# Slot attention's scan: the normalisation of a slot's probabilities moves behind score 2 of the next slot in VectorE's order

## The reference

```python
def step(carry, xs):                       # over 512 tokens, 16 heads, 2 sequences
    Sk, Sv = carry
    q_t, k_t, v_t, w_t, g_t, b_t = xs
    gt = jnp.exp(g_t)
    bw = b_t[:, :, None] * w_t
    Sk = Sk * gt[:, :, None, :] + k_t[..., :, None] * bw[:, :, None, :]
    Sv = Sv * gt[..., None] + bw[..., None] * v_t[:, :, None, :]
    s = jnp.einsum('bhd,bhdm->bhm', q_t, Sk) * SCALE
    a = jax.nn.softmax(s, axis=-1)
    o_t = jnp.einsum('bhm,bhmd->bhd', a, Sv)
    return ((Sk, Sv), o_t)
```

## Time and profile before

| | |
|---|---|
| device time, median of 3 runs | 2822.17 us (2818.21 to 2822.36) |
| the profiled execution | 2818.94 us, of which 2817.0 us are its span |
| granted TensorE clock, mean | 0.935 of full speed |
| busy share PE / PEld / DVE / ACT / POOL | 85% / 59% / 62% / 43% / 36% |
| the four scans | about 205 us each, from 142, 490, 832 and 1176 us of the span |
| in the first scan's window, 142 to 349 us | PE 171, PEld 152, DVE 143, ACT 98, POOL 143 us busy |

### The profile page before, as it was taken

One profiled execution on the slowest core, in us unless ns is written; L12 is line 12 of the kernel. 1 busy time (PEld: TensorE's weight loads), 2 busy tenths in 40 slices (PEclk: granted clock), 3 DMA queues, 4 the chain that ended last, 5 costly groups with the idle time before them and its releaser, 6 DMA issues. The chain is left out here.

```text
span 2817.0 us, 51029 instructions
## 1 busy us (share of the span) xinstructions
PE 2402.7 (85%) x18448; PEld 1654.4 (59%) x18448; DVE 1744.1 (62%) x3466; ACT 1204.1 (43%) x2945; POOL 1022.4 (36%) x1200
## 2 busy tenths in 40 slices
PE   6888788887888878889639999998889769999988
PEld 3377644776457754578526566676533346666675
DVE  3867676775867758677436667632457456766612
ACT  3645445553555534554314444422225334444401
POOL 0177511775227741277304434320120024444300
PEclk9999899998999979999779999998989989999989
DMA  2100001000010000000030000000100130000000
GB/s 51 40 3 2 2 16 34 2 2 2 15 34 2 3 2 15 16 2 2 2 101 18 17 17 17 6 0 1 46 1 1 24 89 18 17 12 10 6 0 15
DMA packets 74983, 46.64 MB, mean 17 GB/s; under 512 B 27416, under 2 KB 68256, under 8 KB 74400
## 3 DMA queue, kind: packets, MB, share of 16 engines
q1 hardware_dynamic: 74784, 43.95, 5.6%
HBM read 42.89 MB, written 1.05 MB: 16 GB/s over the span
## 5 line engine op out<-in xcount | busy, mean ns | idle before, releaser
L1087 DVE SCALAR_TENSOR_TENSOR work<-four,taps,work 128x511 f32<-128x511 f32 (+2 forms) x384 | 284.2, 747 | 119.4 <-ACT work L816 109.2
L1488 POOL TENSOR_TENSOR rot<-q_plain,ropes 128x512 f32<-128x512 f32 x66 | 83.6, 1267 | 707.1 <-ACT q_plain L1510 707.1
L560 PE MATMUL four<-xT,wring 128*128 128x512 f32 x512 | 258.9, 632 | 6.6 <-DMA wring<-in_Ww_dram 4.6
L842 ACT ACTIVATE work<-four 128x512 f32<-128x512 f32 x216 | 129.0, 597 | 272.0 <-PE four L631 245.9
L1459 DVE TENSOR_REDUCE nmaxf<-four 128x1 f32<-128x512 f32 (+3 forms) x256 | 125.7, 491 | 167.2 <-PE four L1385 160.3
L682 PE MATMUL four<-work 128*128 128x128 f32 x1536 | 214.5, 283 | 0.0
L1528 ACT ACTIVATE pr<-four,nmaxf 128x512 f32<-128x512 f32 (+3 forms) x256 | 133.9, 525 | 180.0 <-DVE nmaxf L1459 176.8
L1383 PE MATMUL four<-rot,rot 128*128 128x512 f32 (+3 forms) x512 | 192.4, 472 | 11.8 <-ACT oT L1323 6.1
L682 PEld LDWEIGHTS four<-work 128*128 128x128 f32 x1536 | 191.2, 194 | 3.9
L1013 POOL TENSOR_TENSOR work<-work 128x256 f32<-128x256 f32 x184 | 146.0, 793 | 76.4 <-DVE work L1135 57.5
L716 PE MATMUL bank<-work 128*32 128x16 f32 (+1 forms) x4864 | 99.5, 193 | 84.7 <-POOL work L1020 75.7
(11 more groups left out here) (244 smaller groups left out, 5475.9 us busy)
## 6 DMA issues: line engine op xcount, KB each, us to landing
wqkv<-in_f_wq_dram SPq DMA_DIRECT2D x34, 128.0 KB, 2.2
wqkv<-in_f_wk_dram SPq DMA_DIRECT2D x34, 128.0 KB, 2.3
wqkv<-in_f_wv_dram SPq DMA_DIRECT2D x34, 128.0 KB, 2.3
wo<-in_f_wo_dram SPq DMA_DIRECT2D x2, 2048.0 KB, 10.8
we<-in_f_we_dram SPq DMA_DIRECT2D x4, 1024.0 KB
wring<-in_Ww_dram SPq DMA_DIRECT2D x4, 512.0 KB, 3.9
wring<-in_Wk_dram SPq DMA_DIRECT2D x4, 512.0 KB, 3.8
wring<-in_Wv_dram SPq DMA_DIRECT2D x4, 512.0 KB, 3.8
```

Of the source, the lines that this page charges most:

```text
L560: last = nc.tensor.matmul(k.bank[i % 3][:], wring[n % 2][:, c, h * P:(h + 1) * P], k.xT[:, c, b * T:(b + 1) * T], start=(c == 0), stop=(c ...
L1087: ins = nc.vector.scalar_tensor_tensor(out=cbuf[i % 4][:, s:], in0=k.bank[i % 3][:, 0:T - s], scalar=taps[:, {"q": 0, "k": 1}.get(kind, 2) ...
```

## The change

Two calls change places in DVE's loop of the scan. `normalise(mid)` at j = 2 stood ahead of `score(now, j)`, and now stands behind it. Nothing is added and nothing is removed: the program has the same instructions with the same shapes, and only DVE's order differs, at 28 places (7 slots in 4 groups).

```diff
                             if j == 3 and mid is not None:
                                 first_values(mid)
-                            if j == 2 and mid is not None:
-                                normalise(mid)
                             if now is not None:
                                 score(now, j)
                             if j == LEVELS - 1 and new is not None:
                                 mask_level(new, 0)
+                            if j == 2 and mid is not None:
+                                normalise(mid)
```

## The result

The changed kernel took 2844.14 us in the median of 4 runs (2835.48 to 2848.74), the kernel before 2820.98 us (2818.21 to 2822.36): 1.008 times as long, with a 95% interval of 1.0054 to 1.0106. It is 23 us slower. The profiled execution has a span of 2833.5 us, 16.5 over the 2817.0 of before.

A forecast was written before the change was run, and what follows sets the result against it. No engine is always busy in the scans; a chain of waits through PE bounds them. 16 x 0.50 + 6 x 1.24 + 2 x 0.84 = 17.1 us longer, 2839.3 against the median; range 2825 to 2850.

The forecast's parts named there:

- the mechanism of the wait: In the scans, PE's turned slots would wait for DVE's L1162 at nearly all of the 28 places.
- the sum of 17.1 us: Four scans together longer: 8.0 us from 16 places, 7.4 from 6 and 1.7 from 2.
- The roomy place: 16 places in slots 2 to 7, margin 1.13 to 1.15 us: PE's turned slots start 0.50 us later.
- The bound below, 0.31: Lowest delay of PE's turned slots at the 16 wide-margin places, with L1162 taking 0.69 us free of POOL.
- The tight place: Places with DVE later, margin 0.12 us: turned slots 1.52 us later; 1.24 passes on at 6 places, 0.84 at 2.
- How many are tight: 8 listed places in slots 3, 4, 5 and 7 have DVE later and a margin of 0.12 us.
- The cut at 242.5: Slot 4, first group: DVE and POOL wait for PE, so PE's delay between 237.65 and 241.94 passes to all.
- Slots 1: First slot of each group, 4 places, where DVE waits 2.20 us for exponentials: gain 0, at most 4.8 us.
- rival 1: In the scans, PE starts late but something else sets the pace: 2822 to 2828 us; chance 0.14.
- rival 3: In the scans, POOL sets the pace and pair level 6 starts 0.33 us sooner: 7.9 us faster, 2814.3; chance 0.08.
- Rival 2: At all places the addition loses 0.33 and L1162 0.30 us more to POOL: 29.6 us, 2851.8; chance 0.14.
- the forecast of 2836.0: Whole kernel: the 17.1 us longer set against the profiled execution of 2818.9; against the median it is 2839.3.

The follow-up runs named there:

- mask first: Against the kernel before, only the mask of level 4 goes ahead of the normalisation, product and addition of score 2 stay behind it: 2823.7 us, ratio 0.9996.
- product first: Against the kernel before, mask and product of score 2 go ahead of the normalisation, the addition stays behind: 2829.0 us (1.0025), again 2830.7 us (1.0024).
- late everywhere: The changed kernel with two reductions added on DVE ahead of the reciprocal, delaying the normalised slots at every place: 2908.2 us, 1.0307 against the kernel before.
- slot 1 alone: Against the kernel before, the change is made in slot 1 of each group alone, 4 places of 28: 2822.8 us, ratio 0.9993.

## Why the prediction was right

It said slower by 17.1 us, 9.9 to 24.3 with its bounds; the runs say 23, 22 and 24. Direction, place and the mechanism of the wait are as put down: 2844.1 lies in the range, not at its middle. Part of the time comes from a mechanism that the prediction didn't have. In the three traces of the changed kernel the scans are 19.6, 32.3 and 34.9 us longer, and the 3, 7 and 8 falls of the clock make about 6, 14 and 16 us of that. Without them 14, 18 and 19 us are left, which is what the sum of 17.1 us was about. That the range took in the clock's share as well was luck.

- **The roomy place, 0.50 us.** It measured 0.38 or 0.39. All positions up to L1162 hold to 0.03 us: with 232.64 as the maximum's start the product is at 236.07, the reciprocal at 236.99 and L1162 at 237.21. The difference is L1162's own time beside POOL, 0.78 and not 0.88. The bound below, 0.31, was for a free L1162.
- **The tight place, 1.52 us at the turned slots and 1.24 at the cut.** The late places measured 6.03 against 4.30, so 1.73, since L1162 took 1.11 us beside POOL's L1013 and not 0.88. At the cut, without half speed, pair level 0 stands at 10.30 against 8.90: 1.40. Both are inside the bounds given. By the length of the scans a late place costs 0.36 + 0.9, about 1.3 us, close to the 1.24.
- **How many are tight, 8.** I took the one trace's list as a property of those slots. It isn't: traces with the old DVE order in slots 2 to 7 have 8, 10 and 11 of them, mask first has 2, the changed order has 4, 10 and 11, in other slots each time. Why DVE falls 0.6 us behind ahead of the maximum in one execution and not in another was not found.
- **The cut at 242.5.** Right: the 0.39 us at the turned slots are 0.38 us there and 0.38 in the step.
- **Slots 1, gain 0.** Right, by its own run.
- **The missing term: the clock.** No step of the sum asked what a longer wait does to PE's speed afterwards. It can account for all that the timed runs have over the forecast. The rows of slots 1 could have told: PE waits 3.02 us there in the kernel before, and score 3 behind it takes 1.66 to 1.92 us instead of 1.06.
- **Rivals.** The delay was not taken up (rival 1). POOL does not set the pace (rival 3), though pair level 6 did start 0.32 us sooner, 4.08 for 4.40 after the maximum, as that rival had it. Rival 2's double collision exists, at the late places alone.

The profiled execution at 2835.5 us seems to hit the forecast of 2836.0. That is a coincidence: it had half the late places that I had counted on, and three at a speed that I had not.

## What to carry to other kernels

When an instruction's result is handed to an engine that runs in order, read the margin between the two in the trace before anything is put ahead of it: here it was 1.14 us at an ordinary place, one instruction cost nothing, two cost 5 to 9 us and three cost over 20. Read the margin at all places where the pattern repeats and in more than one execution, since the tight ones move: single traces of the changed kernel showed between 4 and 11 of them. And when a change makes TensorE wait longer, look at the granted clock behind the wait: the half-speed matmuls there can cost more than the wait.

## What the runs showed of the hardware

**The clock can fall after two short waits.** In the changed kernel's traces TensorE stood for 1.23 us, worked 0.68 us, and stood for 1.66 us; at 18 of 25 such places it then ran at the lower level, mostly for the whole of score 3 and what follows. At the 47 ordinary places of those traces, with waits like 0.93 and 0.64 us, it never fell. In product first's second trace it fell at 5 of 10 places with 1.23 and 0.57 us. In the changed kernel with the turned slots behind score 3 it fell at none of 9 places that had these two waits with score 3 between them. In the kernel late everywhere it fell at 8 of 13 places with 0.93 and 1.66 us, and at all 11 with 1.23 and 2.16 to 2.36 us. With one wait of 1.23 or 1.25 us and no second it fell at none of 48 places, in the traces of before and of slot 1 alone. Which of the equal places fall differs from trace to trace, and no row here tells why. The Trainium skill, TensorE: Matmul & The Clock Gate, Part 1, says that the clock goes by how busy the engine has been lately and that the moment varies between runs of one kernel; the traces agree.

**A collision costs nearly what the other has left.** L1162, 128x512 with two SBUF inputs, took 0.69 us alone. It took 1.11 us where POOL's product had 0.57 us left when it began (934.35, POOL's L1013 from 934.25 for 0.67), 0.88 with 0.33 left (235.63, L1013 from 235.04 for 0.92), and 0.78 with 0.23 left (239.77, L1001 from 239.31 for 0.69). Each time it lost 0.14 or 0.15 us less than that. In product first POOL came second: its L1001 began at 237.37 with 0.56 us of the normalisation's product left, and took 1.04 us where it takes 0.62, while the normalisation kept its 0.69. The Trainium skill, SBUF — State Buffer, section "Who interferes with whom", calls the shared ports an exclusive lock and says that the order of issue decides who blocks; the rows fit. That the lock lasts for the whole instruction, as the prediction has it, the page says of the two-port modes alone.

**The stretches between the scans come in steps.** In the kernel before they took 182.2, 174.3 and 178.8 us, in the first trace of the changed one 180.6, 178.6 and 174.3 us. In that trace DVE is busy for the same 118.5 to 118.8 us in all three, while PE is busy for 148.1, 146.0 and 141.9 us at a mean granted clock of 0.88, 0.90 and 0.92. So each stretch can move a run by 4 us or more with the scans as they are. In the four traces with scans of 660 to 662 us the three stretches took 535.3 to 547.5 us in sum, and the spans were 2817.0 to 2827.1 us. That this makes most of the spread of the kernel before, 2813 to 2834 us over 25 runs, is likely but not shown, since one trace of that kernel is all there is.
